# Keys and values of the third narrow attention projected ahead, in the passage from the experts to the wide stage

## The chip, the cores and the metric

One core of one Trainium2 chip (trn2). The metric is the device time of one execution in microseconds (us); three runs of the kernel before were timed, and one more was profiled. Engines: TensorE (PE; PEld is its weight load), VectorE (DVE), ScalarE (ACT), GpSimd (POOL), and SyncE (SP), which issues DMAs. Each has its own queue, worked off in order; they wait for each other by semaphores.

## What is computed

A two-layer decoder on 16 sequences of 64 tokens of 128 features, all f32. Each layer is self attention, cross attention to a context, and a feed-forward part, each followed by a layer norm of the sum with its input:

```python
x = _layernorm(x + _L0_attn_ref(x, ...))          # 16 heads of 8, rotary: "first narrow stage"
x = _layernorm(x + _L0_xattn_ref(x, ctx, mask))   # 16 heads of 8, masked: "second narrow stage"
x = _layernorm(x + _L0_ffn_ref(x, ...))           # 8 experts, the best 2 of each token
x = _layernorm(x + _L1_attn_ref(x, ...))          # 16 heads of 64: "wide stage"
x = _layernorm(x + _L1_xattn_ref(x, ctx, mask))   # 16 heads of 8, masked: "third narrow stage"
x = _layernorm(x + _L1_ffn_ref(x, ...))           # weights rounded to -1, 0, 1, gelu: "ternary stage"
```

The third narrow stage is this (a head has 8 features; its keys and values come from the context alone):

```python
q, k, v = split_heads(x, Wq), split_heads(ctx, Wk), split_heads(ctx, Wv)
scores = jnp.where(mask == 0, -1e12, q @ k.T / sqrt(8))
out = (softmax(scores) @ v) merged @ Wo.T
```

## The kernel before

**Tiles.** The 1,024 tokens are 8 tiles of 128 tokens (two sequences each). Every stage treats a tile as one job. Two streams of jobs exist: `pre` (first and second narrow stage) and `post` (wide, third narrow, ternary: 24 jobs). Between them the experts run (`Routed`). The order of work within a stream is written out by hand in `stream_pe`, `stream_act`, `stream_dve` and `stream_pool` (L1190 to L1337): in step j an engine does one part of the job j, another part of job j-1, and so on back to job j-5. The functions `post_pe` to `post_pool` (L1953 to L1976) add single pieces at a step, "late" ones at its end.

**A narrow job.** `qk_pe` (L500) projects keys and queries on TensorE into two PSUM banks (L514), `qk_dve` (L647) multiplies the keys by the mask (L675) into `KT`, `qk_act` (L601) copies the queries (L618). `blocks_pool` (L695) spreads the keys over heads, so that a matmul with 64 rows gives the scores of eight heads: two GpSimd products of 128x512 a tile into `KB` (L701), each signalled by its own semaphore count. `v_pe` (L521) projects the values in four matmuls (L532), and `v_act` (L623) copies them in two pieces into `VB` (L631). `s_pe` (L538) makes the scores in banks 0 and 1 (L548) and adds the mask's fill (L559); `max_dve` (L398) takes the maximum (L403) and subtracts it (L413, L409 for the wide stage); `exp_act` (L416) takes the exponential (L419). The banks are free for the next job after the subtraction. Then come the transposes of the probabilities (L429, copied by L438), the weighing of the values `va_pe` (L575), the reciprocal and product `y_dve` (L687, L691), a transpose (L591), the output projection (L597), the residual sum and its statistics (`r_dve`, L388, L324), the reciprocal root on GpSimd (L331, L333), the norm (L337) and the transpose of the normed tile (L371, copied by ScalarE, L376).

**A wide job.** Queries and keys are 32 matmul instructions per tile (`qkw_pe`, L812), values 8 (L824), scores 64 (L838), weighed values 64 (L872), output 32 (L856). `fill` (L796) sends the projections through the banks 6, 7 and 4 in turn; ScalarE and VectorE copy them out (L888). VectorE sums the exponentials (L923, L927), and GpSimd multiplies by the reciprocals (`shares_pool`, L917, 128x1024). The norm of a wide tile is VectorE's L337, behind GpSimd's root.

**The passage.** `Routed.pe` (L1632) ends with the transposes of the ternary weights (`fct`, L270), their bias projection (`project_bias`, L992), their means (`means_pe`, L1009, which waits for VectorE's L1000), and the transpose of the first normed tile (`turn_pe`, L1787), which waits for VectorE's L1777. `Routed.act` ends with the copies of `fct`, a small exponential (L1690), and the copy of that tile (L1793). `Routed.dve` ends with `fold` (L997, L1000), `mix_dve` (L1525 to L1529), and for the tiles 0 and 1 `combine` (L1757, L1760 and the statistics L1763, L1765) and `apply` (L1777), then `center` (L1014). GpSimd gathers the experts' rows by indirect DMAs (L1747, two per tile) and makes the roots (L1770, L1772) between them. The tiles 2 to 7 are combined and normed inside the first steps of the stream `post`; the lines that place the last of them are

```python
            if late and j == 3:
                for t in (6, 7):
                    moe.apply(dve, t)
```

`WALL` holds the experts' weights, 12,288 f32 per partition; nothing reads it after the last expert block. `PS` is PSUM, eight banks of 512 f32. `CT` is the context transposed, `WT` the transposed projection weights, `mk` the key mask.

## Time and profile before

| | |
|---|---|
| median of 3 runs | 357.86 us (357.72 to 358.66) |
| the profiled execution | 358.16 us, span 356.2 us |
| instructions | 10,773 |
| PE / PEld busy | 316.5 / 262.3 us (89% / 74%) |
| DVE / ACT / POOL busy | 232.6 / 182.4 / 202.9 us (65% / 51% / 57%) |
| chain that ended last | PE 69%, DVE 14%, ACT 5%, issue 5%, POOL 2%, DMA 2% |
| granted TensorE clock, mean | 0.98 |

How to read it: the span is the time in which engines work, and lies inside the execution's time. The chain is followed back from the last instruction, at each step to what released it; "issue" is time in which an engine waited for nothing that the profile shows. All times in rows are microseconds from the start of the span, of one execution. A number such as "x8" counts instructions: an f32 matmul of the program is two on TensorE. In a row of the timeline, merged instructions have their summed extent, and in brackets stands the idle time before, with what ended it. Granted clock 1.00 is 2.4 GHz, 0.50 is 1.2 GHz.

### The profile page before, as it was taken

Reading aid. Unit: us, or ns where it says so; the run is one execution under the profiler, and the core shown is the slowest. Engines: PE = TensorE matmul, PEld = TensorE weight load, DVE = VectorE, ACT = ScalarE, POOL = GpSimd, SP = SyncE. Lnnn points to the kernel's source line nnn. Section 1 sums busy time; section 2 is a strip of 40 time slices with the busy share of each in tenths; the row PEclk is TensorE's granted clock in tenths of the full one; section 3 lists DMA queues with packets and bytes.
Section 4 is the critical chain, followed back from the end, with each engine's and each line's share of the span. In section 5 each row is a group of like instructions: output and inputs, shape, how many; then the busy total and the mean of one; then the engine's idle time right before and its main releaser. Section 6 shows DMA issues by size and latency. Waiting matters only on the chain.

```text
span 356.2 us, 10773 instructions
## 1 busy us (share of the span) xinstructions
PE 316.5 (89%) x4207; PEld 262.3 (74%) x4207; DVE 232.6 (65%) x554; ACT 182.4 (51%) x384; POOL 202.9 (57%) x289
## 2 busy tenths in 40 slices
PE   3869899998887899999993898899999798999993
PEld 2637667776677799999982876689888666677773
DVE  2699988888855035563334389766555676787685
ACT  2457667776578622323311244354545466677651
POOL 2856998886777255533306675333122464586784
PEclk9989999999999999999997699999999999999999
DMA  6799999000001211111101110000000000000001
GB/s 186 226 300 261 297 326 323 30 3 2 32 29 54 62 44 46 46 45 53 33 22 39 45 31 17 2 4 2 2 4 2 3 4 3 2 2 2 4 22 37
DMA packets 37052, 23.55 MB, mean 66 GB/s; under 512 B 4228, under 2 KB 34956, under 8 KB 36876
## 3 DMA queue, kind: packets, MB, share of 16 engines
q1 hardware_dynamic: 35692, 20.16, 19.9%
q0 software_dynamic: 1024, 2.10, 2.0%
q8 instruction: 34, 0.56, 0.7%
q10 hardware_dynamic: 288, 0.62, 0.5%
q14 instruction: 14, 0.11, 0.1%
HBM read 15.13 MB, written 7.73 MB: 64 GB/s over the span
## 4 chain that ended last, share of the span: by engine, by line
PE 69%; DVE 14%; ACT 5%; issue 5%; POOL 2%; DMA 2%; SPq 1%; POOLq 0%; ACTq 0%; DVEq 0%
PE banks L812 7%; PE banks L429 6%; PE banks L1590 6%; PE banks L1621 6%; PE banks L1598 6%; PE banks L548 6%; PE banks L575 5%; PE banks L856 4%; PE banks L824 3%; PE banks L514 3%; PE banks L872 2%; PE banks L532 2%; DVE mx L403 2%; ACT WALL L1386 2%; PE banks L838 2%
## 5 line engine op out<-in xcount | busy, mean ns | idle before, releaser
L701 POOL TENSOR_TENSOR KB<-KT,cst 128x512 f32<-128x512 f32 x48 | 49.3, 1048 | 7.8 <-DVE KT L661 5.6
L438 ACT ACTIVATE PT<-banks 128x512 f32<-128x512 f32 x64 | 34.8, 595 | 27.0 <-PE banks L429 25.5
L403 DVE TENSOR_REDUCE mx<-banks 128x16 f32<-128x1024 f32 x32 | 38.6, 1206 | 8.7 <-PE banks L559 7.3
L1613 DVE TENSOR_TENSOR PT<-banks,PR 128x512 f32<-128x512 f32 x23 | 15.9, 691 | 39.4 <-PE banks L1598 35.1
L888 ACT ACTIVATE U<-banks 128x512 f32<-128x512 f32 x44 | 26.1, 597 | 30.2 <-PE banks L812 15.4
L1578 POOL COPY U<-WALL 128x1024 f32 x21 | 21.9, 1043 | 34.1 <-PE banks L1598 33.9
L331 POOL TENSOR_SCALAR ve<-mv 128x1 f32<-128x1 f32 x40 | 9.2, 230 | 46.3 <-DVE mv L326 45.6
L429 PE MATMUL banks<-cst,PR 128*128 128x128 f32 x256 | 34.2, 277 | 1.5 <-POOL PR L917 1.5
L419 ACT ACTIVATE PR<-PR 128x1024 f32<-128x1024 f32 x32 | 33.9, 1058 | 3.1 <-DVE PR L413 2.6
L812 PE MATMUL banks<-XT,WQKV 128*128 128x128 f32 x256 | 33.6, 294 | 0.4 <-ACT XT L1793 0.4
L812 PEld LDWEIGHTS banks<-XT,WQKV 128*128 128x128 f32 x256 | 32.0, 207 | 1.1 <-ACT XT L1793 0.7
L429 PEld LDWEIGHTS banks<-cst,PR 128*128 128x128 f32 x256 | 28.8, 143 | 3.9 <-POOL PR L917 2.3
L548 PE MATMUL banks<-KB,QS 64*64 64x512 f32 x192 | 28.1, 634 | 2.9 <-DVE PR L413 2.2
L413 DVE TENSOR_TENSOR PR<-banks,mx 128x1024 f32<-128x1024 f32 x24 | 29.4, 1225 | 0.8
L575 PE MATMUL banks<-VB,PT 128*64 128x18 f32 x768 | 26.0, 210 | 0.0
L1747 POOL DMA_INDIRECT KB<-routed_rows,pos x16 | 16.0, 998 | 16.4 <-DMA routed_rows<-YS 12.3
L575 PEld LDWEIGHTS banks<-VB,PT 128*64 128x64 f32 x768 | 24.4, 138 | 1.2 <-issue 0.3
L917 POOL TENSOR_TENSOR PR<-PR,rs 128x1024 f32<-128x1024 f32 x8 | 15.2, 1904 | 17.1 <-DVE rs L927 17.0
L1621 PE MATMUL banks<-WALL,PT 128*128 x184 | 24.4, 276 | 0.6 <-DVE YS L1629 0.6
L1590 PE MATMUL banks<-XGT,U 128*128 128x128 f32 x184 | 24.5, 276 | 0.5 <-ACT XGT L1568 0.5
L333 POOL TENSOR_TENSOR rstd<-ve,half 128x1 f32<-128x1 f32 x40 | 23.0, 575 | 3.3
L1598 PE MATMUL banks<-XGT,U 128*128 128x128 f32 x184 | 24.3, 275 | 0.0
(192 smaller groups left out, 727.1 us busy)
## 6 DMA issues: line engine op xcount, KB each, us to landing
routed_rows<-zero SPq DMA_DIRECT2D x1, 4544.0 KB, 19.5
WALL<-in_L_ffn_wg_dram SPq DMA_DIRECT2D x8, 256.0 KB, 5.3
WALL<-in_L_ffn_wu_dram SPq DMA_DIRECT2D x8, 256.0 KB, 5.5
WALL<-in_L_ffn_wd_dram SPq DMA_DIRECT2D x8, 256.0 KB, 5.8
U<-in_L_attn_W_qkv_dram SPq DMA_DIRECT2D x1, 1536.0 KB, 22.5
XG<-routed_rows SPq DMA_DIRECT2D x23, 64.0 KB, 1.8
routed_rows<-YS SPq DMA_DIRECT2D x23, 64.0 KB, 1.6
cst<-shape_constants ACTq DMA_DIRECT2D x1, 537.0 KB, 4.5
```

The costliest lines, as they stand in the source:

```text
L403: dve.tensor_reduce(mx[:, n % 2, :], s, AX.X, ALU.max).then_inc(self.max.sem, 1)
L413: dve.tensor_tensor(PR[:, n % 2, :].rearrange("q (h k) -> q h k", k=SEQ), s, bc(mx[:, n % 2, :], 2, SEQ), ALU.subtract).then_inc(self.sub. ...
L419: act.activation(p, p, ACT.Exp, scale=self.scale).then_inc(self.exp.sem, 1)
L429: t = pe.transpose(PS[:, B_PT + m, P * (r % 4):P * (r % 4 + 1)], PR[:, n % 2, P * r:P * (r + 1)], ident)
L438: act.activation(PT[:, n % 2, 4 * m:4 * m + 4, :].rearrange("p r q -> p (r q)"), PS[:, B_PT + m, :], ACT.Copy).then_inc(self.pt.sem, 1)
L548: pe.matmul(PS[q, B_S + g, :], QS[f, n % 3, q], KB[f, n % 2, b].rearrange("p h k -> p (h k)"), start=True, stop=False)
L575: m = pe.matmul(PS[64 * b:64 * b + 64, B_Y, w * r:w * (r + 1)], PT[:, n % 2, r, 64 * b:64 * b + 64], VB[:, n % 3, r, b].rearrange("p a e - ...
L701: pool.tensor_tensor(KB[:, n % 2, b], bc(KT[:, n % 2, b, :], 1, 8), bc(cst[:, C_HEAD:C_HEAD + 8], 2, SEQ), ALU.mult).then_inc(self.kb.sem, 1)
L812: m = pe.matmul(PS[:, bank, P * k:P * (k + 1)], WQKV[:, f // 2, P * u:P * (u + 1)], XT[:, P * i:P * (i + 1)], start=True, stop=True)
L1590: m = pe.matmul(PS[:, j % 2, P * c:P * (c + 1)], WE[:, j % 3, 0, P * c:P * (c + 1)], XGT[:, j % 3, :], start=True, stop=True)
L1598: m = pe.matmul(PS[:, 2 + j % 2, P * c:P * (c + 1)], WE[:, j % 3, 1, P * c:P * (c + 1)], XGT[:, j % 3, :], start=True, stop=True)
L1621: m = pe.matmul(PS[:, 7, 0:P], HT[:, j % 2, c, :], WALL[:, e, 2, P * c:P * (c + 1)], start=(c == 0), stop=(c == CH - 1))
```

## The change

The keys and values of the third narrow stage depend on the context alone. The change makes them for all eight tiles in the passage and keeps them in the free `WALL`: masked keys in `KTA`, values in `VCA`. TensorE gets two matmuls of 512 columns (after `project_bias`) and 32 of 64x64 (after `means_pe`); VectorE two products (after `mix_dve`), ScalarE four copies (ahead of `turn_act`). GpSimd makes the key blocks `KBA`, one tile at the end of each step 3 to 10 of the stream `post`, in 16 products as before. In the third narrow stage `qk_pe` projects queries only, `v_pe`, `qk_dve` and `blocks_pool` do nothing, `v_act` copies from `VCA` instead of PSUM, and `s_pe` reads `KBA`, both halves behind one semaphore. Two waits are new on TensorE in the wide stage: the kept values ahead of the third fill of the first tile, whose bank they used, and the kept keys ahead of its scores.

```diff
         WSWAP = region(9216, 1024, "p (u f) -> p u f", u=PAIRS)
+        WFREE = WALL[:, :, :, :].rearrange("p e w i -> p (e w i)")
+        KBA = WFREE[:, 0:8192].rearrange("p (t b h k) -> p t b h k", t=NT, b=2, h=8)
+        KTA = WFREE[:, 8192:9216].rearrange("p (t b k) -> p t b k", t=NT, b=2)
+        VCA = WFREE[:, 9216:10240].rearrange("p (t c) -> p t c", t=NT)
...
-            def __init__(self, name, w, src, rope=False, bias=None, fill=None, row=None, next_row=None):
-                self.w, self.src, self.rope, self.bias, self.fill = w, src, rope, bias, fill
+            def __init__(self, name, w, src, rope=False, bias=None, fill=None, row=None, next_row=None, ahead=False):
+                self.w, self.src, self.rope, self.bias, self.fill, self.ahead = w, src, rope, bias, fill, ahead
...
                 self.norm.xr = Mark("bias_added", NT if next_row is not None else 0)
+                if ahead:
+                    self.ka_mm, self.ka = Mark("keys_projected_ahead", 2), Mark("keys_kept", 2)
+                    self.va_mm, self.vc = Mark("values_projected_ahead", 2), Mark("values_kept", 4)
+                    self.kba = Mark("k_blocks_made_ahead", NT)
+            def keys_ahead_pe(self, pe):
+                for g in range(2):
+                    pe.matmul(PS[:, g, :], WT[:, self.w + 1, :], self.src[:, BANK * g:BANK * (g + 1)],
+                              start=True, stop=True).then_inc(self.ka_mm.sem, 1)
+            def values_ahead_pe(self, pe):
+                for g in range(2):
+                    for t in range(4):
+                        for b in range(2):
+                            for a in range(2):
+                                c = P * t + 64 * b
+                                m = pe.matmul(PS[64 * a:64 * a + 64, 3 + g, c:c + 64],
+                                              self.src[:, SEQ * (2 * (4 * g + t) + b):SEQ * (2 * (4 * g + t) + b + 1)],
+                                              WT[:, self.w + 2, :].rearrange("f (r a d) -> f a r d", a=2, d=DH)[:, a],
+                                              start=True, stop=True)
+                    m.then_inc(self.va_mm.sem, 1)
+            def keys_ahead_dve(self, dve):
+                for g in range(2):
+                    dve.wait_ge(*self.ka_mm.at(g + 1))
+                    dve.tensor_tensor(KTA[:, 4 * g:4 * g + 4].rearrange("p t b k -> p (t b k)"), PS[:, g, :],
+                                      mk[:, 4 * g:4 * g + 4, :].rearrange("p t k -> p (t k)"), ALU.mult).then_inc(self.ka.sem, 1)
+            def values_ahead_act(self, act):
+                for g in range(2):
+                    act.wait_ge(*self.va_mm.at(g + 1))
+                    for a in range(2):
+                        rows = slice(64 * a, 64 * a + 64)
+                        act.activation(VCA[rows, 4 * g:4 * g + 4].rearrange("p t c -> p (t c)"), PS[rows, 3 + g, :],
+                                       ACT.Copy).then_inc(self.vc.sem, 1)
+            def blocks_ahead_pool(self, pool, i):
+                pool.wait_ge(*self.ka.at(i // 4 + 1))
+                pool.tensor_tensor(KBA[:, i, 0], bc(KTA[:, i, 0, :], 1, 8), bc(cst[:, C_HEAD:C_HEAD + 8], 2, SEQ), ALU.mult)
+                pool.tensor_tensor(KBA[:, i, 1], bc(KTA[:, i, 1, :], 1, 8), bc(cst[:, C_HEAD:C_HEAD + 8], 2, SEQ), ALU.mult)\
+                    .then_inc(self.kba.sem, 1)
...
             def qk_read(self, i):
+                if self.ahead:
+                    return [self.q_ready.at(i + 1)]
...
                         pe.wait_ge(*s)
-                for bank, w, src, s in ((B_K, 1, self.src, self.k_mm), (B_Q, 0, XT, self.q_mm)):
+                both = ((B_K, 1, self.src, self.k_mm), (B_Q, 0, XT, self.q_mm))
+                for bank, w, src, s in both[1:] if self.ahead else both:
...
                 i = job.i
+                if self.ahead:
+                    return
...
                 for b in range(2):
-                    pe.wait_ge(*self.kb.at(2 * i + b + 1))
+                    if self.ahead:
+                        pe.wait_ge(*self.kba.at(i + 1))
+                    else:
+                        pe.wait_ge(*self.kb.at(2 * i + b + 1))
+                    k = KBA[:, i, b] if self.ahead else KB[:, n % 2, b]
...
                         f = slice(64 * g, 64 * g + 64)
-                        pe.matmul(PS[q, B_S + g, :], QS[f, n % 3, q], KB[f, n % 2, b].rearrange("p h k -> p (h k)"),
+                        pe.matmul(PS[q, B_S + g, :], QS[f, n % 3, q], k[f].rearrange("p h k -> p (h k)"),
...
             def v_read(self, i):
-                return [self.v_ready.at(i + 1)]
+                return [] if self.ahead else [self.v_ready.at(i + 1)]
...
                 i, n = job.i, job.n
-                act.wait_ge(*self.v_mm.at(i + 1))
+                act.wait_ge(*(self.vc.at(4) if self.ahead else self.v_mm.at(i + 1)))
...
                     rows = slice(64 * a, 64 * a + 64)
+                    src = VCA[rows, i, :] if self.ahead else self.v_at(job, rows, None)
                     m = act.activation(VB[rows, n % 3, :, :, a, 0:DH].rearrange("p r b d -> p b r d"),
-                                       self.v_at(job, rows, None).rearrange("p (b r d) -> p b r d", b=2, d=DH), ACT.Copy)
+                                       src.rearrange("p (b r d) -> p b r d", b=2, d=DH), ACT.Copy)
...
                     return
+                if self.ahead:
+                    return
...
                 i, n = job.i, job.n
+                if self.ahead:
+                    return
...
                 for f in range(4):
+                    if i == 0 and f == 2:
+                        pe.wait_ge(*a2.vc.at(4))
...
                     pe.wait_ge(*job.before.s_read())
+                else:
+                    pe.wait_ge(*a2.ka.at(2))
...
                 fc.project_bias(pe)
+                a2.keys_ahead_pe(pe)
                 fc.means_pe(pe)
+                a2.values_ahead_pe(pe)
...
                 act.activation(pk[:, 1, :], pk[:, 0, :], ACT.Exp).then_inc(self.e2.sem, 1)
+                a2.values_ahead_act(act)
...
                 self.mix_dve(dve)
+                a2.keys_ahead_dve(dve)
...
         wide.input = moe.norm
-        a2 = Narrow("cross1", 8, CT, fill=1, next_row=2)
+        a2 = Narrow("cross1", 8, CT, fill=1, next_row=2, ahead=True)
...
         def post_pool(pool, j, late):
+            if late and 3 <= j < 3 + NT:
+                a2.blocks_ahead_pool(pool, j - 3)
...
```

## Rows read from the trace of the kernel before

**Rows 1.** The page, busy time of each engine
```profile
PE 316.5 (89%) x4207; PEld 262.3 (74%) x4207; DVE 232.6 (65%) x554; ACT 182.4 (51%) x384; POOL 202.9 (57%) x289
```

**Rows 2.** Stretches: length, busy PE, PEld, DVE, ACT, POOL, granted clock, DMA share, GB/s
```profile
184.00:192.00 8.00, 4.70 (x34) 3.74 (x33) 2.99 (x12) 2.09 (x3) 2.70 (x3) 1.00 0.12 34
192.00:202.00 10.00, 6.16 (x28) 5.90 (x29) 3.56 (x11) 1.66 (x4) 7.67 (x11) 0.50 0.15 40
```

**Rows 3.** Instructions in order of time, the passage: start us, us, engine line [idle before]
```profile
187.88 1.13 PE L992 MATMUL banks<-FCT,PT 128*128 128x128 f32 x8 [0.87 <-DVE FCT L283]
...
190.25 1.16 PE L1009 MATMUL banks<-FCT,PT 128*128 128x128 f32 x8 [1.24 <-DVE FCT L1000]
...
192.69 0.35 DVE L1757 SCALAR_TENSOR_TENSOR R<-KB,pk,X 128x128 f32<-128x128 f32 x1 [1.98 <-DMA KB<-routed_rows,pos]
...
195.47 0.45 PE L1787 MATMUL banks<-cst,X 128*128 128x128 f32 x1 [4.07 <-DVE X L1777]
```

**Rows 4.** The chain of waits, first wide projections: start us, us, what
```profile
196.29 6.70 PE banks L812 x32
...
205.01 3.77 PE banks L812 x32
```

**Rows 5.** The chain of waits, prices in the last stages
```profile
310.76 0.45 PE banks L514 x4
...
312.30 0.38 PE banks L532 x8
...
341.59 0.86 PE banks L1037 x2
```

**Rows 6.** The page, costliest groups: ScalarE's copies from PSUM
```profile
L888 ACT ACTIVATE U<-banks 128x512 f32<-128x512 f32 x44 | 26.1, 597 | 30.2 <-PE banks L812 15.4
```

**Rows 7.** Instructions in order of time, GpSimd, first wide steps
```profile
202.62 0.95 POOL L1747 DMA_INDIRECT KB<-routed_rows,pos  x1 [0.30 <-issue]
204.99 0.28 POOL L1770 TENSOR_SCALAR ve<-mv 128x1 f32<-128x1 f32 x1 [1.42 <-DVE mv L1765]
...
207.24 1.07 POOL L1747 DMA_INDIRECT KB<-routed_rows,pos  x1 [0.17 <-issue]
...
217.28 1.91 POOL L917 TENSOR_TENSOR PR<-PR,rs 128x1024 f32<-128x1024 f32 x1
```

**Rows 8.** Instructions in order of time, norms on VectorE behind a root on GpSimd
```profile
224.18 0.34 DVE L1777 TENSOR_SCALAR X<-R,mv,rstd 128x128 f32<-128x128 f32 x1 [0.77 <-POOL rstd L1772]
...
300.09 2.05 POOL L701 TENSOR_TENSOR KB<-KT,cst 128x512 f32<-128x512 f32 x2
300.16 1.06 DVE L337 TENSOR_SCALAR X<-R,mv,rstd 128x128 f32<-128x128 f32 x1 [0.78 <-POOL rstd L333]
```

**Rows 9.** Instructions in order of time, VectorE in a wide step
```profile
234.45 1.22 DVE L923 TENSOR_REDUCE mx<-PR 128x16 f32<-128x1024 f32 x1 [0.53 <-ACT PR L419]
...
238.22 1.28 DVE L888 COPY U<-banks 128x512 f32<-128x512 f32 x2
```

**Rows 10.** The chain of waits, wide steps and the change of stages
```profile
240.54 1.75 PE banks L856 x32
...
279.86 1.89 issue
```

**Rows 11.** Instructions in order of time, third narrow stage
```profile
306.04 0.30 PE L591 MATMUL banks<-cst,ysb 128*128 128x128 f32 x1 [0.66 <-ACT XT L376]
...
309.19 1.09 PE L548 MATMUL banks<-KB,QS 64*64 64x512 f32 x8
...
310.54 1.23 DVE L403 TENSOR_REDUCE mx<-banks 128x16 f32<-128x1024 f32 x1 [0.65 <-PE banks L559]
...
311.80 1.23 DVE L413 TENSOR_TENSOR PR<-banks,mx 128x1024 f32<-128x1024 f32 x1
...
316.17 2.04 POOL L701 TENSOR_TENSOR KB<-KT,cst 128x512 f32<-128x512 f32 x2
...
317.93 1.41 PE L548 MATMUL banks<-KB,QS 64*64 64x512 f32 x8
```

## Prediction

> **What bounds the kernel now.** First the page's busy times: TensorE is busy for 316 of 356 us [rows 1], so work taken off TensorE pays wherever its queue is full, and only there. Then TensorE's granted clock through the passage from the experts to the wide stage: at its full level of 2.4 GHz until 192, at its half level of 1.2 GHz for ten microseconds from then on [rows 2]. It fell just after TensorE had run out of work, and came back after it had again worked without a break. Then the instructions of the passage: the bias projection L992 begins at 187.88, the means L1009 at 190.25, and then comes nothing until the first transpose of a normed tile, L1787, at 195.47, which waits for gathered rows [rows 3]. VectorE is idle too, for 1.98 us up to 192.69 [rows 3]. Then the chain of waits: the first wide projection takes 6.70 us at half clock, the second 3.77 us at full clock, for the same 32 instructions [rows 4]. From about 230 the chain is TensorE alone, 10.7 us per wide tile, until the wide stage ends near 300; the third narrow stage follows, two tiles in 8.7 us [rows 10, 11].
>
> **Part A, the passage.** Added on TensorE: two key projections of 512 columns, each like L1037, 0.86 us [rows 5], so 1.72 us; they go in after L992, 189.0 to 190.75. The means then begin 0.5 us late, end near 191.7, and nothing here waits for them soon. The 32 value matmuls are eight times the group L532 at 0.38 us [rows 5]: 3.04 us, 191.7 to 194.8. The transpose at 195.47 is not delayed, with 0.7 us of cover; without that cover each microsecond would go straight into the first wide projection.
> VectorE gets two 128x512 products from PSUM; its nearest rows are two copies of that size in 1.28 us [rows 9]. I take 1.4 us in all, inside its idle 1.98 us [rows 3]; the second ends near 192.2. ScalarE gets four copies of 512 columns, at 597 ns each by L888 [rows 6]: the second pair runs 194.9 to 196.05, while the copy of the transposed tile behind it (L1793) would start at 195.96. That costs 0.1 us. No DMA is added or moved, so SP's queue is untouched.
> What this buys is clock. TensorE now has work from 187.9 to 194.8 with no gap, so I take it that the full clock stays. The first wide projection then takes 3.8 us rather than 6.70, and ends 2.8 us earlier [rows 4]. Not all of that lasts. GpSimd issues the gathers one after another, and the one of 202.62 does not move with TensorE. Behind it GpSimd now idles for 1.42 us, until VectorE, held up behind the slow projection, has the statistics of tile 2; the next gather is issued at 207.24 [rows 7]. With the projection early, that idling and 0.2 us of the same behind it go: the gather is issued near 205.6. From there to the first shares product L917, now at 217.28 [rows 7], are 10.04 us, of which about 0.8 are again idling for VectorE's statistics and go too: 205.6 + 10.04 - 0.8 = 214.85. So 2.45 us of the 2.8 last; the bounds are 1.6 (the gather's own shift) and 2.8.
> Against it stands the first pair of key blocks, which GpSimd now starts right behind the reciprocal root of expert tile 7, in the same moment in which VectorE wants to norm that tile (L1777 at 224.18, 0.34 us, on the chain) [rows 8]. The trace has this meeting: at 300.09 the blocks L701 start behind a root, and VectorE's tensor_scalar L337 of 300.16 takes 1.06 us instead of 0.34 [rows 8]. So +0.7 us (bounds 0, if VectorE is first, and 1.7, if it waits out both blocks). Part A: 2.45 - 0.7 = **1.75 us**.
> The Trainium skill ("SBUF — State Buffer", section "SBUF: two separate sides") has the rule that speaks against this change: GpSimd and a two-port VectorE instruction exclude each other for the whole instruction, whoever starts first. The trace agrees with it, in the row of 300.16. By the rule alone the price at 224 is 0 or the rest of one block, and the sum would be 0.7 us better if VectorE came first.
>
> **Part B, wide steps and the change of stages.** GpSimd makes two blocks (2.05 us [rows 8]) in each of the steps 3 to 10, right behind the root of the wide tile before. The norm L337 is then stretched by 0.7 us in each. The sum L923 behind it waits for ScalarE's exponential 0.53 us anyway, so VectorE's chain slips 0.2 us; the second copy L888, ending at 239.50 now, has 1.0 us in hand before TensorE wants it for L856 at 240.54 [rows 9, 10]. Cost 0 while TensorE is full. Only in the next to last wide step does TensorE wait for VectorE (1.89 us from 279.86 [rows 10]): there the 0.2 us is paid. At the change of stages the chain holds the key half of one L514 group (0.45/2 = 0.22 us) and two value groups L532, 0.38 us each [rows 5]. Part B: 0.22 + 0.38 + 0.38 - 0.2 = **0.8 us**.
>
> **Part C, around 304.** The transpose L591 at 306.04 has waited 0.66 us for a copy on ScalarE [rows 11], which stands behind two value copies and an exponential; the value copies in turn wait there for L532. With the values kept since the passage they wait for nothing, and TensorE gets to its tile transpose 0.6 us (0.22 + 0.38) sooner, so the copy comes about 0.7 us earlier: **0.7 us**. (The copies themselves stay: from SBUF instead of PSUM. L888 and the exponentials give no difference that I can see; I take 0, at most 0.05 us each.)
>
> **Part D, the steady steps.** From L548 at 309.19 to L548 at 317.93 are two steps, 4.37 us each [rows 11]. The change takes 0.22 (keys) and 0.38 (values) off a step: 3.77. But the score banks make a loop. L548 begins at 309.19, the maximum L403 (1.23 us) at 310.54, the subtraction L413, as long again, at 311.8, and with it and the hand-over the next L548 could start at 313.1, 3.9 us after the last [rows 11]. So 3.9 is the new period and not 3.77, and VectorE is **late next**: two steps give 8.74 - 7.8 = 0.94. The step of 317.93 gives its 0.38 (it projects no keys any more) and 0.3 more: its L548 takes 1.41 instead of 1.09 us, because the key blocks begun at 316.17 end at 318.2 [rows 11]. With the loop again the limit I take 0.65. The last step gives 0.38, and the part from 306.04 to 309.19 gives 0.6. Part D: 0.94 + 0.65 + 0.38 + 0.6 = **2.55 us**. VectorE's eight L675 and GpSimd's blocks leave too, but they only lay beside. The last stage shifts unchanged.
>
> **Sum.** 1.75 + 0.8 + 0.7 + 2.55 = 5.8 us off. The profiled execution took 358.16 us (span 356.2), the median of the runs is 357.86; the difference of 0.3 I keep. 358.16 - 5.8 - 0.3 = 352.1; I write 352.2.
>
> **Rivals.**
> 1. *The clock does not help.* It falls in the gaps that are left (194.8 to 195.47, and from 195.8 to 196.4), or the gathers hold the pace alone. For it: gaps and a half clock lie side by side in this passage [rows 2, 3]. Against: the clock stayed full from 184 to 192, when TensorE had gaps as well [rows 2]. The 2.45 us fail: 352.2 + 2.45 = 354.65. Chance 0.14.
> 2. *The third narrow stage is held by others.* VectorE's order puts the residual sum, its statistics and a normalization between two maxima, and ScalarE's exponential stands behind its other copies. Against: L403 at 310.54 had waited for TensorE [rows 11]. If the period only comes down to 4.2, Part D gives 0.9 and C 0.3: 354.2. Chance 0.14.
> 3. *Everything comes.* VectorE wins the race at 224, the 2.8 us last, the period is 3.77: 0.7 + 0.35 + 0.5 more, 350.65. Chance 0.06.
> 4. *Slower.* The place is VectorE's norm in the wide steps, seven of which count. If a norm and the sum after it are held 2.45 us (both blocks, 2.05, and 0.2 at either end for the hand-overs), 0.53 and 1.0 us are slack and 0.9 us goes onto TensorE per step: 6.4 us, plus 1.75 in Part A. 352.2 + 8.2 = 360.4. It costs TensorE anything at all from a hold of 1.5 us on, and makes the kernel slower than before from about 2.15 (seven steps and Part A then give back the 5.8). Against: the L337 that met blocks took 1.06 us, no more [rows 8]. Chance 0.04.
> The change could also fail to act, by its new waits on the kept values ahead of the third fill; those values are out 2 us before. I give that nothing of its own.
>
> **Numbers.** Forecast 0.62, rivals 0.14, 0.14, 0.06, 0.04. The range reaches from the third to the first and the second with half a microsecond beyond: 350.3 to 355.3, which leaves out both together (356.7) and the fourth. About 0.3% (1.07 us) can be told from no change. Only the fourth and a pile of bad bounds end above 356.8: faster 0.94, same 0.02, slower 0.04.
>
> **What would show it.** Full clock in every stretch from 188 to 206, and a first L812 group of 3.8 us; L917 near 214.9; L1777 of tile 7 and the L337 of the wide steps at 1.06 us with wide steps still 10.7 us; no L701, no L675 of the third narrow stage; L548 to L548 3.9 us, with VectorE in the chain between. A first L812 group over 6 us, wide steps over 10.8 us or narrow steps over 4.1 us would prove the step in question wrong.

## The result and the profile after

The changed kernel takes **355.20 us** (median of 7 runs, 353.66 to 356.67); the kernel before takes 357.80 beside it (7 runs, 356.67 to 358.66). The ratio is 0.9931 with a 95% interval of 0.9909 to 0.9953: 2.6 us or 0.7% faster. 352.2 was predicted, a gain of 5.7 us on the 357.86 known then. The direction was right, the size was not: less than half of the gain came, and the median lies just inside the range.

The profiled execution of the changed kernel is the fastest of its seven, 353.66 us (span 351.3); that of the kernel before, 358.16, is slower than all but two of the seven beside it. So this pair shows 4.5 us, far more than the medians, and has to be read with care. The page of the kernel after:

```profile
span 351.3 us, 10723 instructions
PE 312.0 (89%) x4195; PEld 258.4 (74%) x4195; DVE 236.0 (67%) x548; ACT 183.9 (52%) x388; POOL 202.2 (58%) x289
PEclk9999999999999999999999999999999989999998
PE 61%; DVE 19%; ACT 6%; issue 6%; DMA 3%; POOL 3%; SPq 1%; POOLq 0%; ACTq 0%; DVEq 0%
```

TensorE is busy for 4.5 us less than in [rows 1]. One slice with a lower clock stands late, at 281 to 290. The instructions of the passage, in order of time (start us, us, engine, line, what, idle before):

```profile
187.98 1.88 PE L488 MATMUL banks<-CT,WT 128*128 128x512 f32 x4
...
189.83 1.28 DVE L508 TENSOR_TENSOR WALL<-banks,mk 128x512 f32<-128x512 f32 x2
...
190.68 2.08 PE L498 MATMUL banks<-WT,CT 128*64 128x64 f32 x64
...
191.88 2.44 ACT L517 ACTIVATE WALL<-banks 64x512 f32<-64x512 f32 x4 [4.20 <-PE banks L498]
...
194.50 0.30 PE L1860 MATMUL banks<-cst,X 128*128 128x128 f32 x1 [1.74 <-DVE X L1850]
...
195.17 3.84 PE L879 MATMUL banks<-XT,WQKV 128*128 128x128 f32 x32 [0.37 <-ACT XT L1866]
...
199.12 0.96 POOL L1820 DMA_INDIRECT KB<-routed_rows,pos  x1 [0.30 <-issue]
...
202.35 0.35 DVE L1830 SCALAR_TENSOR_TENSOR R<-KB,pk,X 128x128 f32<-128x128 f32 x1 [1.42 <-DMA KB<-routed_rows,pos]
```

The first wide projection takes 3.84 us instead of 6.70 [rows 4], at 2.4 GHz. But the values are through in 2.08 us, not 3.04, so TensorE stands idle for 1.74 us before the transpose, where the forecast left it 0.7 us. And after the quick projection VectorE waits 1.42 us for gathered rows (those of tile 3; its second gather is the L1820 of 199.12). The norms that meet the key blocks on GpSimd, and the first shares product (L986, once L917):

```profile
213.91 1.91 POOL L986 TENSOR_TENSOR PR<-PR,rs 128x1024 f32<-128x1024 f32 x1
...
220.80 1.05 DVE L1850 TENSOR_SCALAR X<-R,mv,rstd 128x128 f32<-128x128 f32 x1 [0.76 <-POOL rstd L1845]
...
230.83 1.04 POOL L523 TENSOR_TENSOR WALL<-WALL,cst 128x512 f32<-128x512 f32 x1
230.90 1.06 DVE L342 TENSOR_SCALAR X<-R,mv,rstd 128x128 f32<-128x128 f32 x1 [1.00 <-POOL rstd L338]
```

The chain of waits from the change of stages on (start us, us, what; here a row begins where the one before it ends, so it can start a little later than in the timeline):

```profile
274.16 0.93 PE banks L941 x64
275.09 1.87 PE banks L891 x8
276.96 2.33 issue
279.29 3.00 PE banks L925 x32
282.29 1.61 PE banks L434 x8
...
306.15 1.02 PE banks L608 x8
310.01 1.09 PE banks L608 x8
314.05 1.02 PE banks L608 x8
317.92 1.09 PE banks L608 x8
```

Narrow steps are 3.86, 4.04 and 3.87 us apart, as forecast. The chain has TensorE alone in them. But the forecast loop of the score banks closes too: in order of time, each score group begins 0.1 us after VectorE's subtraction L418 (once L413) has ended.

```profile
308.69 1.22 DVE L418 TENSOR_TENSOR PR<-banks,mx 128x1024 f32<-128x1024 f32 x1
...
310.01 1.09 PE L608 MATMUL banks<-WALL,QS 64*64 64x512 f32 x8
...
312.62 1.23 DVE L418 TENSOR_TENSOR PR<-banks,mx 128x1024 f32<-128x1024 f32 x1
...
313.98 1.09 PE L608 MATMUL banks<-WALL,QS 64*64 64x512 f32 x8
```

New is what stands at 277: TensorE waits 2.33 us, not 1.89 [rows 10], and the two groups behind it take 3.00 and 1.61 us; in the wide steps of the same trace they take 1.97 and 1.02. The stretches show what goes with it (length, busy PE, PEld, DVE, ACT, POOL, granted clock, DMA share, GB/s):

```profile
279.00:281.00 2.00, 1.71 (x23) 1.74 (x25) 0.19 (x1) 0.00 (x0) 0.00 (x0) 0.76 0.04 8
281.00:283.00 2.00, 2.00 (x17) 1.67 (x14) 0.59 (x2) 0.00 (x0) 0.00 (x0) 0.50 0.00 0
```

The clock fell to 1.2 GHz right behind TensorE's wait. In the page of the kernel before it did not.

To see what is luck, each trace is cut at three marks: the first gather of the passage, the first output projection of the wide stage, and the first matmul of the ternary stage. That gives four pieces. In the profiled pair the first piece, in which nothing was changed, differs by 0.86 us (188.69 to 187.83), the second goes from 41.04 to 39.23 and the third from 97.12 to 94.83. So the passage gives 1.81, as forecast, the third piece 2.29 of the 4.05 us of Parts B, C and D, and 0.86 is chance.

### The profile page after: what moved, and what is told of

The parts are those of the page before. It is cut to its first block, busy times and chain, and to the rows that moved or that the text cites. A ratio compares the mean times of both kernels' runs of the same rounds, so it can differ in the third digit from the quotient of the medians.

```text
span 351.3 us, 10723 instructions
## 1 busy us (share of the span) xinstructions
PE 312.0 (89%) x4195; PEld 258.4 (74%) x4195; DVE 236.0 (67%) x548; ACT 183.9 (52%) x388; POOL 202.2 (58%) x289
## 4 chain that ended last, share of the span: by engine, by line
PE 61%; DVE 19%; ACT 6%; issue 6%; DMA 3%; POOL 3%; SPq 1%; POOLq 0%; ACTq 0%; DVEq 0%
PE banks L1659 6%; PE banks L1690 6%; PE banks L1667 6%; PE banks L434 6%; PE banks L608 5%; PE banks L925 5%; PE banks L635 4%; PE banks L879 4%; DVE mx L408 3%; PE banks L891 3%; ACT WALL L1455 2%; PE banks L1106 2%; PE banks L941 2%; DVE PR L418 2%; PE banks L568 2%
## 5 line engine op out<-in xcount | busy, mean ns | idle before, releaser
L766 POOL TENSOR_TENSOR KB<-KT,cst 128x512 f32<-128x512 f32 x32 | 32.9, 1048 | 6.1 <-DVE KT L722 5.8
L879 PE MATMUL banks<-XT,WQKV 128*128 128x128 f32 x256 | 30.7, 278 | 0.4 <-ACT XT L1866 0.4
L418 DVE TENSOR_TENSOR PR<-banks,mx 128x1024 f32<-128x1024 f32 x24 | 29.4, 1225 | 0.8
L879 PEld LDWEIGHTS banks<-XT,WQKV 128*128 128x128 f32 x256 | 29.2, 192 | 1.0 <-ACT XT L1866 0.6
L1820 POOL DMA_INDIRECT KB<-routed_rows,pos x16 | 15.9, 991 | 16.4 <-DMA routed_rows<-YS 12.3
L1690 PEld LDWEIGHTS banks<-WALL,PT 128*128 128x128 f32 x184 | 22.4, 192 | 0.8 <-issue 0.8
L1659 PEld LDWEIGHTS banks<-XGT,U 128*128 128x128 f32 x184 | 22.4, 192 | 0.7 <-issue 0.7
```

Source lines behind the costliest of these rows:

```text
L418: dve.tensor_tensor(PR[:, n % 2, :].rearrange("q (h k) -> q h k", k=SEQ), s, bc(mx[:, n % 2, :], 2, SEQ), ALU.subtract).then_inc(self.sub. ...
L766: pool.tensor_tensor(KB[:, n % 2, b], bc(KT[:, n % 2, b, :], 1, 8), bc(cst[:, C_HEAD:C_HEAD + 8], 2, SEQ), ALU.mult).then_inc(self.kb.sem, 1)
L879: m = pe.matmul(PS[:, bank, P * k:P * (k + 1)], WQKV[:, f // 2, P * u:P * (u + 1)], XT[:, P * i:P * (i + 1)], start=True, stop=True)
L1659: m = pe.matmul(PS[:, j % 2, P * c:P * (c + 1)], WE[:, j % 3, 0, P * c:P * (c + 1)], XGT[:, j % 3, :], start=True, stop=True)
L1690: m = pe.matmul(PS[:, 7, 0:P], HT[:, j % 2, c, :], WALL[:, e, 2, P * c:P * (c + 1)], start=(c == 0), stop=(c == CH - 1))
```

## The experiments

Two theories. **Clock by luck**: the added matmuls in the passage (below: the filling) often do not hold the clock, and the longer wait at the change of stages costs a fall of its own. **Gathers**: GpSimd's gathers and its blocks hold the pace in the passage, whatever the clock does. All medians below are of 6 to 12 runs; a ratio is to the kernel before, run beside it, with its 95% interval.

**The changed kernel once more** (`again`, no edit).

> The changed kernel unchanged, for its spread and for a second trace. Theory (clock): the seven runs so far follow their mean granted clock, 353.7 us at 0.991 and 356.7 us at 0.981; the new ones fall on the same line, and a trace with a lower mean clock shows one or two more stretches of about 3.4 us at the half level than the trace at hand (which has one, 280 to 283.5, besides the last microseconds). Rival (something else varies, for instance the gathers' landing): times that differ by 1 us or more at equal mean clock, and differences in waits at full clock. Ratio to the kernel before near 0.993 either way.

Measured: 354.95 us (12 runs), ratio 0.9934 [0.9909, 0.9959]; profiled 356.38. In this trace the clock falls in both places. Its chain:

```profile
196.82 5.47 PE banks L879 x32
...
281.93 3.16 PE banks L925 x32
285.09 1.45 PE banks L434 x8
```

and the stretch in which the first projection stands (columns as above; the clock is the last but two):

```profile
197.00:200.00 3.00, 3.00 (x16) 3.00 (x17) 1.00 (x3) 0.60 (x1) 2.44 (x4) 0.53 0.17 46
```

The same code, and 5.47 us instead of 3.84 for the first projection, with TensorE idle for 1.76 us ahead of the transpose, as in the other trace (1.74). So the same code either keeps the clock in the passage or loses it; the fall at the change of stages came again. The clock is not all that varies: four of the twelve runs have a mean clock of 0.981, and their times go from 355.15 to 356.38 us, which is what the rival named.

**Eight matmuls nobody reads, in the wait at the change of stages** (`fill_at_change`).

```diff
         def post_pe(pe, j, late):
+            if j == 9 and not late:
+                pe.wait_ge(*wide.norm.r.at(5))
+                pe.wait_ge(*wide.norm.xev.at(4))
+                for _ in range(8):
+                    pe.matmul(PS[:, B_OX, 0:P], ident, ident, start=True, stop=True)
```

> Eight f32 matmuls of 128 columns (1.8 us) on TensorE inside the wait of 2.3 us ahead of the output projection in step 9, into an unused part of a bank. Theory (TensorE's stop at the change of stages lets the clock fall, and that took back 1.6 us of the gain): full clock from 280 to 284 in the trace, L925 there 2.0 and L434 1.0 us instead of 3.0 and 1.6, and a median 1 to 1.6 us below the changed kernel's. Rival (the fall of the clock is a thing of this one execution's phase and mostly lies elsewhere): median within 0.5 us of the changed kernel's, mean clocks spread as before.

Measured: 353.38 us, 0.9885 [0.9852, 0.9918]. The chain:

```profile
279.38 1.98 PE banks L2031 x16
281.36 0.34 issue
281.70 1.97 PE banks L925 x32
283.67 1.02 PE banks L434 x8
```

With TensorE kept busy the clock stays, and the two groups are back at 1.97 and 1.02. The third piece of the trace is 93.23 us, against 94.82 of `again`: 1.6 us, the price of that fall. The median is 1.6 us lower as well, as the theory had it, which is more than this fall can give if it comes in some executions only; six runs against twelve leave room for that.

**Key blocks moved behind the shares product** (`blocks_after_shares`): GpSimd makes them after the softmax share, not behind the root.

```diff
         def post_pool(pool, j, late):
-            if late and 3 <= j < 3 + NT:
-                a2.blocks_ahead_pool(pool, j - 3)
+            if not late and 4 <= j < 4 + NT:
+                a2.blocks_ahead_pool(pool, j - 4)
```

> The key blocks are issued on GpSimd behind the shares product of the steps 4 to 11, not behind the root of the steps 3 to 10; nothing else is changed. Theory (a block and VectorE's norm exclude each other): every L342 of the wide steps and the L1850 of tile 7 take 0.35 us again instead of 1.06, the first output projection of the wide stage comes 0.7 us earlier, TensorE's wait in step 9 shrinks from 2.3 to 2.1 us; 0.7 to 0.9 us less in all. Rival (the hold is hidden, since the chain at 220 has another limit): norms 0.35 us, but the same total within 0.3 us.

Measured: 353.28 us, 0.9899 [0.9861, 0.9937]; the profiled execution took 351.11. VectorE's norms in order of time:

```profile
220.66 0.35 DVE L1850 TENSOR_SCALAR X<-R,mv,rstd 128x128 f32<-128x128 f32 x1 [0.77 <-POOL rstd L1845]
...
230.04 0.35 DVE L342 TENSOR_SCALAR X<-R,mv,rstd 128x128 f32<-128x128 f32 x1 [1.00 <-POOL rstd L338]
```

and the chain at the change of stages:

```profile
276.11 2.11 issue
278.22 1.97 PE banks L925 x32
280.19 1.02 PE banks L434 x8
```

The hold is gone from both norms (0.35, not 1.05 and 1.06), the wait at the change shrinks from 2.33 to 2.11 as the 0.2 of Part B says, and the clock does not fall. This execution is at full clock from the passage to the last stage. The median is 1.7 us below that of `again`, where 0.7 to 0.9 was expected; the norm and the shorter wait account for 0.9, the rest is not shown. A fall that stays away at the shorter wait would give it.

**The kernel before with the filling alone** (`before_busy_passage`): TensorE does the key and value projections in the passage, and nothing reads them; everything else is as before.

```diff
                 fc.project_bias(pe)
+                for g in range(2):
+                    pe.matmul(PS[:, g, :], WT[:, 9, :], CT[:, BANK * g:BANK * (g + 1)], start=True, stop=True)
                 fc.means_pe(pe)
+                for k in range(16):
+                    for a in range(2):
...
```

> The kernel before, with the 2 and 32 matmuls of the passage added on TensorE as pure filling: their results are read by nobody, and the third narrow stage is as before. It tells the clock's part from the moved work's part. Theory (the clock held through the passage is worth 2.45 us, as Part A has it): 2 to 2.5 us below the kernel before, first wide projection 3.8 us, first shares product 2.4 us earlier. Rival (the gathers set the pace): first projection 3.8 us, but the first shares product moves by under 1 us and the total stays within 0.5 us.

Measured: 356.95 us, 0.998 [0.9955, 1.0004]. Its stretches:

```profile
194.00:198.00 4.00, 1.85 (x25) 1.55 (x22) 2.06 (x8) 0.28 (x1) 2.87 (x5) 1.00 0.13 32
198.00:201.00 3.00, 3.00 (x18) 3.00 (x17) 0.94 (x2) 1.20 (x2) 2.40 (x5) 0.54 0.09 26
```

The first projection takes 5.48 us. The filling delays and shortens the fall (3.4 us at the lower level, where the three traces of the kernel before have 10.2, 6.9 and 10.2), but does not exclude it. So neither expectation was met as it stands, since both had the projection at 3.8 us. The second piece is 39.62 us against the 41.04 of the first trace before.

**More matmuls in the passage** (`fill_passage`).

```diff
                 a2.values_ahead_pe(pe)
                 pe.wait_ge(*fc.bias.at(1))
+                for _ in range(6):
+                    pe.matmul(PS[:, 7, 0:P], ident, ident, start=True, stop=True)
                 self.turn_pe(pe, (0,))
+                for _ in range(1):
+                    pe.matmul(PS[:, 7, 0:P], ident, ident, start=True, stop=True)
```

> The changed kernel with six f32 matmuls of 128 columns (1.3 us) on TensorE between the last value projection and the first transpose of the passage, and one behind it. Theory (in the executions where the clock still falls after the passage, TensorE's stop of 1.7 us before that transpose is the reason): no stretch at the half level between 186 and 206 in the trace, median 0.5 to 1 us below the changed kernel's 355.15, mean clock up by about 0.004. Rival (the fall comes from something else, or the filling delays the transpose): the clock falls there as often as before, or the transpose comes later than 6.6 us after the first gather; no gain.

Measured: 354.61 us, 0.9929 [0.9903, 0.9954]: no clear gain over the 354.95 of `again`, which belongs to another set. The clock holds in the passage, the second piece is 39.56. At the change TensorE waits 2.32 us here too, and this time the clock stays: a wait of that length does not always bring the fall. In this trace the clock fell at 220 instead.

**Both fillings, and the blocks moved** (`both_fills_blocks_moved`; the three edits above together).

> The changed kernel with both fillings and with the key blocks behind the shares product in the steps 4 to 11. Theory: the three effects add; only the first transient near 25 us and the tail are left at the half level, mean clock 0.993 or more, median 352.0 to 352.5, that is 5 us below the kernel before and 3 below the changed kernel, and the times spread over less than 2 us. Rival (the fillings only shift where the clock falls): median near 353.3, as with one of them alone.

Measured: 353.20 us, 0.9886 [0.9860, 0.9912]. The 352.0 to 352.5 of the theory did not come; the rival's 353.3 did. Full clock in the passage, yet its piece is 39.27 us, 1.0 longer than in `blocks_after_shares`, which had full clock there too. VectorE, in order of time:

```profile
204.54 0.35 DVE L1834 SCALAR_TENSOR_TENSOR R<-KB,pk,X 128x128 f32<-128x128 f32 x1 [2.19 <-DMA KB<-routed_rows,pos]
```

The rows for tile 3 are late: they landed 3.86 us after the issue of their gather, and VectorE waited 2.19 us for them; in `blocks_after_shares` it was 2.71 and 0.98 us. So what a full clock in the passage gives hangs on when these rows land.

**Keys ahead, values as before** (`keys_only`). Value projections, their copies and their waits go back to the narrow steps.

```diff
             def v_pe(self, pe, job):
                 i = job.i
-                if self.ahead:
-                    return
...
                 fc.means_pe(pe)
-                a2.values_ahead_pe(pe)
                 pe.wait_ge(*fc.bias.at(1))
```

> The changed kernel with the keys projected ahead but the values projected in the third narrow stage as before. It parts the saving there. By Parts B, C and D the values carry 0.76 (change of stages), 0.7 (ScalarE around 300) and some 1.2 us of the steady steps (their 0.38 is partly covered by the loop of the score banks): a steady step of 4.1 us instead of 3.9, and from the last wide step to the first ternary step about 2.7 us more than the changed kernel; at equal clock 355.0 against 352.3. Rival (the loop and VectorE set the pace, keys and blocks were the point): steady step 3.9 to 3.95, total within 1 us of the changed kernel at equal clock.

Measured: 358.12 us, 1.0021 [0.9999, 1.0044], no faster than the kernel before. Its chain:

```profile
279.75 2.33 issue
282.07 2.73 PE banks L921 x32
284.81 1.87 PE banks L434 x8
...
310.75 1.02 PE banks L606 x8
314.84 1.02 PE banks L606 x8
319.04 1.02 PE banks L606 x8
```

Narrow steps come to 4.09 and 4.20 us, the third piece to 97.67, against 94.82 in `again`, which has the fall at the change too. So the values carry 2.85 us (2.7 was expected), and the keys alone about 1.0 (97.05 of the kernel before + 1.6 for the fall − 97.67). That is less than the port hold (0.7) and the fall (1.6) take away.

**The kernel before, twice** (`before_again`, `third_before`; no edit).

> The kernel before, for a second trace of its clock. Theory (the passage always lets the clock fall, and only for how long differs with the phase): half level again from about 192 or 195 on, for 7 or 10 us, no fall at the change of stages (TensorE waits 1.9 us there, less than the changed kernel's 2.3). Rival: a fall at the change of stages here too, so that the changed kernel's is nothing new.

> The kernel before once more, for the third trace. Theory (its wait of 1.9 us there does not let the clock fall, or seldom): 97.0 to 97.1 us from the first wide output projection to the first ternary matmul, as in the other traces of it. Rival (the fall depends on the phase alone): 98.6 us here or there. The first wide projection takes 5.3 to 6.7 us, as the phase has it. Median near 357.2.

Measured: 357.15 us (0.9996 [0.9979, 1.0013]) and 357.31 us (0.9993 [0.9976, 1.0010]). The clock falls in the passage in both, and at the change in neither. The first projection takes 5.35 and 6.70 us: the price of the fall was not always the 2.9 us which the prediction read from one trace. By the first gather as zero the first shares product (L917, L986 in the changed kernel) comes at 27.23 and 28.43 us in these two traces; the trace of the prediction has 28.59.

**Blocks moved, eight matmuls at the change** (`blocks_moved_fill_at_change`), **sixteen transposes at the change** (`transposes_at_change`), and **the changed kernel a third time** (`third_after`). The first joins two edits above; the second has `for _ in range(16): pe.transpose(PS[:, B_OX, 0:P], ident, ident)` as its filling.

> The key blocks behind the shares product in the steps 4 to 11, and the eight filling matmuls in TensorE's wait of step 9; nothing in the passage. Theory (the filling in the passage cost what it gave, the other two effects are independent): median 352.0 to 352.5, about 1 us below either alone (353.3), from the first gather to the first wide output projection 38.3 us (39.3 where the clock falls in the passage), and 93.0 us from there to the first ternary matmul in every trace. Rival (moving the blocks already shortens the wait enough that the clock stays): median 353.2 again.

> The changed kernel with 16 transposes (1.8 us) in place of the eight matmuls in the wait of step 9. Theory (any work on TensorE holds the clock there): as with the matmuls, median 353.4 and 93.2 us from the first wide output projection to the first ternary matmul. Rival (transposes do not count as work for the clock, as the Trainium skill's page on TensorE has it): as without a filling, median near 355.1, and the clock at its half level from 280 to 284 with 94.8 us for that part in most executions.

> The changed kernel once more, for the third trace. Theory (its wait of 2.3 us at the change of stages lets the clock fall in most executions): 94.8 us from the first wide output projection to the first ternary matmul, with L925 near 3 us. Rival (both traces so far were chance): 93.2 us. Median near 355.1 either way.

Measured: 353.27 us (0.9891 [0.9857, 0.9925]), 353.72 us (0.9887 [0.9860, 0.9915]) and 353.52 us (0.9890 [0.9865, 0.9916]). The clock stays at the change in the traces of the two fillings (L925 in 1.97 us), but in this set the changed kernel itself was as fast as they, against both sides of its expectation (median near 355.1): its trace has 3.84 us in the passage, no fall at the change, and on VectorE, in order of time,

```profile
204.86 0.35 DVE L1830 SCALAR_TENSOR_TENSOR R<-KB,pk,X 128x128 f32<-128x128 f32 x1 [2.27 <-DMA KB<-routed_rows,pos]
```

once more the wait for gathered rows. So the medians of this set do not tell a filling from none, and the 352.0 to 352.5 expected of the first of them did not come either.

**Last set**: the changed kernel (`fourth_after`), the blocks moved (`blocks_again`), the filling alone (`before_busy_again`), each as above.

> The changed kernel for the fourth time, beside the two below. In three sets its medians were 355.2, 354.95 and 353.5 against 357.8, 357.1 and 357.4 of the kernel before. Theory (the phase of the clock and the landing of the gathers scatter its executions over 3 us and more, and six to twelve executions don't fix the median to better than 0.7 us): median between 353.5 and 355.3; from the first gather to the first wide output projection 39.2 to 40.3 us, 93.2 or 94.8 us from there to the first ternary matmul. Rival (each chip has its own level): a median outside that.

> The blocks behind the shares product once more. Theory: 0.7 us less than the changed kernel up to the first wide output projection and 0.2 us less behind it, so about 1 us below fourth_after in the median; 38.3 to 39.6 us and 93.0 us for the two parts. Rival (its 353.3 was luck, the hold costs nothing): equal medians within 0.3 us.

> The kernel before with the busy passage once more, for what the clock alone is worth on average. The first time it gave 0.6 us in the mean (356.6 against 357.3), against the 2.45 of Part A. Theory (most of what the clock gives in the passage is given back, as the clock falls for a shorter time there in most phases and VectorE then waits for the rows of tile 3): again 0.4 to 0.9 us below the kernel before in the mean, from the first gather to the first wide output projection 38.5 to 39.7 us. Rival (Part A was right on average): 2 us below.

Measured: 355.55 us (0.9961 [0.9940, 0.9982]), 353.70 us (0.9908 [0.9874, 0.9943]) and 356.72 us (0.9987 [0.9959, 1.0015]). `fourth_after` falls in both places (5.43 us in the passage; third piece 94.81). `blocks_again` has full clock in the passage and VectorE waiting 2.49 us for rows of tile 3 (they landed 4.21 us after the issue), and its clock fell at 219; its second piece is 40.61 us, outside the 38.3 to 39.6 expected. The median of `fourth_after` lies outside the 353.5 to 355.3 expected, on the rival's side. `before_busy_again` has the fall in the passage (5.46 us) and gains 0.5 us in the mean, as expected. With the set of `again`, moving the blocks is worth 1.7 and 1.85 us on the changed kernel: a version that beats both kernels, at 353.3 and 353.7 us.

## Why the prediction was right and where it failed

The measured gain is 2.6 us beside the kernel before, and 2.2, 3.9 and 1.5 in the three later sets that had both. Pooled over all sets, the kernel before has a mean of 357.2 us (121 runs), the changed one 355.0 (37 runs): a gain of 2.2.

**Parts B, C and D were right.** Together 0.8 + 0.7 + 2.55 = 4.05 us were forecast. The third piece goes from 97.05 or 97.06 (four of the five traces of the kernel before, with its filling or without; the profiled one has 97.12) to between 93.0 and 93.5 in all eight traces of the changed stages in which the clock holds: some 3.85 us. By stretch, of the last trace before and `third_after`: 2.0 us up to the first steady score group (forecast 0.8 + 0.7 + 0.6), then 0.84 (0.94), 0.65 (0.65) and 0.34 (0.38). From start to start the steady steps are 3.93 and 3.96 to 3.97 us in every trace that has both keys and values ahead (forecast 3.9). The loop of the score banks is there, with 0.1 us from the subtraction to the next scores, but TensorE is also busy through the first two steps, with 3.86 of 3.86 and 4.04 of 4.04 us. Which of the two sets the pace is not separated, except ahead of 317.92, where TensorE stops for 0.12 us behind the subtraction. The value copies on ScalarE take 0.30 and 0.32 us from SBUF, 0.27 and 0.29 before, inside the 0.05 each that was allowed. The wide step stays at 10.7 us. Rival 2 is out.

**Part A failed in its term for the clock**: "so I take it that the full clock stays", and "2.45 us" of it that last. Up to the first shares product, where the prediction counted them, the kernel before takes 28.59, 27.23 and 28.43 us from the first gather, the changed one 26.08, 27.10, 26.98 and 26.99: 1.3 us less on average, not 2.45. Three things stood against the term.
1. "0.38 us" for a group of values was 0.26. The values were through 4.9 us after the first gather, not 6.1, and the gap ahead of the transpose was 1.7 us, not 0.7. The clock then fell in 7 of the 11 traces that have the filling of the change alone in the passage (first projection 5.43 to 5.48 us), and stayed in 4 (3.84). Without that filling, or with its keys alone, it fell in all four. Where more matmuls closed the gap (`fill_passage`, `both_fills_blocks_moved`) it stayed in both; two traces do not prove that the gap was the cause.
2. Where it stays, the gathers take part of it back, or all. The prediction rightly left the gathers up to 202.62 where they were (tile 3's second one is issued 11.2 to 11.4 us after the first in every trace), but it gave VectorE, which now comes to tile 3 earlier, no wait for the rows. VectorE waits 1.0 to 2.5 us for them in the six traces with full clock there, and in none with the fall. Of the changed kernel's two traces with full clock, one has a second piece of 39.23 us, 1.0 less than those with the fall, the other 40.15, the same.
3. The 6.70 us was read from one trace; the kernel before takes 6.70 twice and 5.35 once.

The filling alone makes the second piece 39.6 us (two traces) instead of 40.5 (three traces: 41.04, 39.68, 40.88): 0.9 us; in the runs' medians 0.2 and 0.4. The changed kernel, with the port hold, averages 39.95 (39.23, 40.26, 40.15, 40.15): 0.6 us gained, not 1.75, which is the 1.3 less the 0.7 of the hold. Of the 2.45 us that rival 1 takes away, about half failed. That the profiled pair shows 1.81 was luck: it sets a long fall against none.

**The port hold was right**: 1.05 us on the last expert tile's norm and 1.06 in the wide steps, and 0.35 as soon as the blocks are moved. The Trainium skill ("SBUF — State Buffer", section "SBUF: two separate sides") says that GpSimd and a VectorE instruction in a two-port mode shut each other out for the whole of the instruction that starts first. The trace agrees, with 1.06 against 0.35 us and a block of 1.04 that began 0.07 us earlier. Rivals 3 and 4 are out.

**A loss that no part held.** Part B put down 0.22 us for the key projection taken off the chain at the change of stages and 0.2 for the held norm. Both are there, but both are also time in which TensorE is idle in its longest wait: 1.89 + 0.22 + 0.2 = 2.31, measured 2.33. At 1.89 us the clock fell in none of 5 traces; at 2.11, with the blocks moved, in none of 2; at 2.3, without filling, in 4 of 6 (3 of the 4 of the changed kernel); filled, in none of 4. That makes it likely, not certain, that the longer wait brings the fall and that filling keeps it off. A fall costs 1.6 us, so 1.2 on average by the changed kernel's traces. This loss stood in no rival.

**The basis** was 0.6 us too high: 357.86 was the median of three runs, 357.2 that of all 121. Ends are compared in pairs on one chip, so this moves the forecast time and not the gain.

In sum: 0.6 + 3.85 − 1.2 = 3.25 us by the traces, and 2.2 by the pooled runs. The rest can be followed. The first piece, in which nothing was changed, happens to be 0.15 us longer in the changed kernel's four traces (188.94 against 188.79), and the ternary stage takes 29.42 us, not 29.35. The time of an execution outside its span is 2.35 us in these traces, not 2.0 (over all runs that list both 2.27 against 1.99); why is open, and no part of the sum had it. That leaves 2.7 us between the traced executions, and those of the kernel before were slow draws: 357.75 us in the mean, against 357.2 of all its runs, with 355.1 against 355.0 for the changed one. Four traces are few for a share of 3 in 4. The clock fell in other places too: near 220 in two traces, between 36 and 103 in four. Not tried: issuing the gather of tile 3 earlier, which would tell what the passage gives once its rows are there.

## What to carry to other kernels

Work taken off a busy engine's path also lengthens the waits that it stood in. Look at the longest remaining idle time of TensorE: a clock that fell there took back 1.6 us of some 3.85 here. When filling is to hold a clock, price it by instructions of the same shape in the same back-to-back order, and look past the filled gap for the next thing late, here a gather. And judge by the pieces of several traces: one profiled pair gave the passage its forecast 1.8 us, four traces against three give it 0.6.

## What the hardware did that was not expected

- The same code has its first wide projection in 3.84 or in 5.47 us, after TensorE stopped for 1.74 and for 1.76 us. In all eleven traces with this filling the stop was 1.68 to 1.86 us.
- A kernel of 355 us varies by 2 to 4.6 us within a set of runs. In the changed kernel's first seven this goes along with the mean granted clock of the execution, from 353.66 us at 0.991 to 356.67 at 0.981; in `third_after` it does not (352.54 at 0.986, 354.54 at 0.990).
- 64-row value matmuls back to back: 64 instructions in 2.08 us, 0.26 per eight, where groups of eight between other work take 0.38 [rows 5].
- Sixteen transposes in TensorE's wait kept the clock up, in the one trace that there is (1.90 us, L925 in 1.97 behind them). The Trainium skill ("TensorE: Matmul & The Clock Gate", section "Part 4: PE-mode transpose") says that transposes don't count as busy in the same way. This trace speaks against it without settling it, since the clock also stayed up in two of the six traces with nothing there.
- Rows gathered by GpSimd land 2.5 us after issue in the median of the first trace after; the ones that VectorE waits for in the passage took 3.15 us there, and 2.71, 3.86 and 4.21 in three others. Why these are later isn't known.
